# Keys and weights laid out by the host part, the order of all engines made anew, and matmuls that nothing reads ahead of the second group

## The reference, cut to what matters

```python
x = x + xattn0(ctx, layernorm(x), mask, b)     # 8 heads of 16: keys ctx[..., :128], values ctx[..., 128:]
x = x + ffn0(layernorm(x), k0, k1, k2, s0, s1, s2)          # 128 -> 512 -> 512 -> 128, weights +1/-1, relu * 2
x = x + xattn1(layernorm(x), ctx, lens, W_in, b_in, g_res, g_init)   # rmsnorm, W_in; picks a decayed patch row of ctx
x = x + ffn1(layernorm(x), W, b, Wg, bg)                    # 8 experts, the best 2 by softmax weigh in
```

## Time and profile before

| | before |
|---|---|
| time, median of 3 runs (lowest to highest) | 539.25 us (538.83 to 540.79) |
| profiled execution: its time, its span | 538.97 us, 537.2 us |
| PE, DVE, POOL, ACT busy | 497.7, 433.1, 364.5, 356.7 us |
| granted PE clock, mean | 0.982 of full speed |

### The profile page before, as it was taken

How to read it: one execution, slowest core, us unless ns; L and a number is a source line. 1 busy time by engine, 2 the same in 40 slices (tenths; PEclk the granted TensorE clock), 3 DMA queues, 4 the chain that set the end, 5 groups by cost and what they waited for, 6 DMA issues and landing times.

```text
span 537.2 us, 15110 instructions
## 1 busy us (share of the span) xinstructions
PE 497.7 (93%) x5549; PEld 324.0 (60%) x5549; DVE 433.1 (81%) x1404; ACT 356.7 (66%) x761; POOL 364.5 (68%) x633
## 2 busy tenths in 40 slices
PE   1756999999999999999999999999999999999893
PEld 1645565666656565766666566666666666655551
DVE  4735868899897979888897979799887785867897
ACT  3398698887967867677686866777566665655410
POOL 7644444588858869686868778686845857654865
PEclk9987899999999999999999999999999999999997
DMA  7402101010310101010110101000000000100010
...
DMA packets 28503, 16.98 MB, mean 32 GB/s; under 512 B 3687, under 2 KB 28429, under 8 KB 28430
## 3 DMA queue, kind: packets, MB, share of 16 engines
q1 hardware_dynamic: 26670, 15.57, 10.5%
...
## 4 chain that ended last, share of the span: by engine, by line
PE 64%; DVE 5%; issue 1%; ACT 0%; DVEq 0%
PE ps L2186 16%; PE ps L2134 16%; PE ps L2145 4%; PE ps L2079 4%; PE ps L2022 4%; PE ps L2096 4%; PE ps L2127 4%; PE ps L2164 2%; PE ps L2165 2%; PE ps L2104 2%; PE ps L2054 2%; PE ps L2177 2%; DVE weighed L1046 1%; PE ps L2083 1%; PE ps L2047 1%
## 5 line engine op out<-in xcount | busy, mean ns | idle before, releaser
L2186 PE MATMUL ps<-w_moeT,y4T 128*128 128x512 f32 x256 | 123.5, 607 | 1.2 <-DVE gd L1005 1.1
L613 POOL TENSOR_TENSOR sum<-weighed 128x512 f32<-128x512 f32 x60 | 76.1, 1269 | 71.2 <-DVE weighed L1046 71.2
L2134 PE MATMUL ps<-h,w 128*128 128x512 f16 x512 | 118.6, 379 | 0.0
L1638 ACT ACTIVATE h<-ps 128x512 f16<-128x512 f32 x128 | 74.1, 591 | 46.9 <-PE ps L2134 35.9
L1046 DVE TENSOR_TENSOR weighed<-ps,wgt 128x1024 f32<-128x1024 f32 x64 | 77.8, 1218 | 31.7 <-PE ps L2186 30.7
L969 DVE SCALAR_TENSOR_TENSOR h<-ps,h 128x512 f16<-128x512 f32 x128 | 85.6, 682 | 20.2 <-ACT h L1638 20.1
L2134 PEld LDWEIGHTS ps<-h,w 128*128 128x128 f16 x512 | 48.3, 98 | 56.2 <-issue 5.6
L1604 ACT ACTIVATE prT<-ps,maskT 77x1024 f32<-77x1024 f32 x64 | 67.3, 1101 | 14.8 <-PE ps L2083 14.5
L2186 PEld LDWEIGHTS ps<-w_moeT,y4T 128*128 128x128 f32 x256 | 45.1, 189 | 43.0 <-issue 35.0
L565 POOL TENSOR_TENSOR rs<-ve,neg_half 128x4 f32<-128x4 f32 x64 | 64.9, 1013 | 8.7
L560 POOL TENSOR_TENSOR ve<-mv,eps 128x4 f32<-128x4 f32 x64 | 14.2, 222 | 60.6 <-DVE mv L903 60.4
...
## 6 DMA issues: line engine op xcount, KB each, us to landing
...
xa<-in_x SPq DMA_DIRECT2D x16, 256.0 KB, 3.0
out_x<-xo SPq DMA_DIRECT2D x16, 256.0 KB, 2.3
...
k_u<-in_L_ffn_k ACTq DMA_DIRECT2D x1, 256.0 KB, 3.9
...
```

What stands on the lines that cost most here:

```text
L613: nc.gpsimd.tensor_tensor(sum4[:], both[:, 0:4 * D], both[:, 4 * D:8 * D], ALU.add).then_inc(c_sum4.sem, 1)
L1638: last = nc.scalar.activation(h[:, 0, (k - 1) % FC, :], src, ACT.Relu)
L2134: last = pe.matmul(pb(g, k), w2[:, i, c * 128:(c + 1) * 128], h1[:, g.p, part, i, :], start=(i == 0 and part == 0), stop=(i == FC - 1 and ...
L2186: last = pe.matmul(pm(g, j)[:, half, :], y4T[:, g.p, j * S:(j + 1) * S], w_moeT[:, half * 512:(half + 1) * 512], start=True, stop=True)
```

## The change

`kernel()` now lays out the inputs on the host: x and the output group by group, each row of a group in one piece of 2 KB; the keys of a group already turned, with zeros in the places of the other head of a pair; the values already padded, with the column of ones; the mask also turned; the expert, projection and gate weights turned and joined in one matrix, their biases in one row.

```diff
+    for h in range(H):
+        keys[:, h, :, h % HR] = grouped[..., h * HD:(h + 1) * HD].transpose(0, 3, 2, 1)
+    values[..., 0:HD] = grouped[..., D:].reshape(NG, NK, G, H, HD)
+    values[..., HD] = 1.0
+    weights = np.concatenate([w.transpose(2, 0, 1).reshape(D, -1), a["L1_xattn_W_in"].T, a["L1_ffn_Wg"].T], axis=1)
...
+            def load_keys(g):
+
+                if g.has(2):
+                    sp.wait_ge(a_less[1].sem, a_less[1].of(g, back=2))
+                sp.dma_start(kT[:, g.p], keys[g.n]).then_inc(keys_in[g.p].sem, 16)
+
+            def load_values(g):
+
+                if g.has(2):
+                    sp.wait_ge(a_pv.sem, a_pv.of(g, back=2))
+                sp.dma_start(vx[:, g.p], values[g.n]).then_inc(values_in[g.p].sem, 16)
```

```diff
+            def a_normalise(g):
+
+                dve.wait_ge(ln_a.rs.sem, ln_a.rs.of(g))
...
+                for j in range(G):
+                    last = nc.vector.tensor_scalar(xn[0][:, g.p, j * D:(j + 1) * D], xa[:, g.f, j * D:(j + 1) * D],
+                                                   mv[0][:, g.p, j, 0:1], rs[0][:, g.p, j:j + 1], ALU.subtract, ALU.mult)
+                last.then_inc(a_xn_v.sem, 1)
```

The last two groups' sums are done otherwise: DVE adds the experts of j = 1, 3 of group 14 and j = 2, 3 of group 15 one by one into the output; for j = 1 of group 15 ACT weighs, PE adds by matmuls with the identity (`e_sum`), ACT takes the result out:

```diff
+        def how(g):
+            return {NG - 2: ("gpsimd", "vector", "gpsimd", "vector"), NG - 1: ("gpsimd", "scalar", "vector", "vector")}.get(g.n, ("gpsimd",) * G)
...
+            def e_accumulate(g, j, half):
...
+                for e in range(4 * half, 4 * half + 4):
+                    so_far = xo if e else xd
+                    if e:
+                        dve.wait_ge(v_step.sem, v_steps(g, j) + e)
+                    last = nc.vector.scalar_tensor_tensor(xo[:, g.p, cols], pm(g, j)[:, e // 4, (e % 4) * D:(e % 4 + 1) * D],
+                                                          wgt[:, g.p, j, e:e + 1], so_far[:, g.p, cols], ALU.mult, ALU.add)
```

```diff
-            a_turn_keys(g[0])
+            keep_busy(12, 4)
             turn_ends()
+            keep_busy(6, 4)
             a_turn_rows(g[0])
+            keep_busy(4, 4)
             a_scores(g[0], 0)
...
-            keep_busy(4, 0)
             d_turns(g[15], (c_yT, g[15]))
-            keep_busy(4, 1)
             d_gate_scores(g[15], (c_x3, g[15]))
-            keep_busy(3, 0)
```

More of the change, by code:

```diff
@@ L60, in turned_at, with build @@
         return self.turned.of(g, self.k, back)
-def build(nc, x, ctx, mask, lens, b_attn, k0, k1, k2, s0, s1, s2, w_in, b_in, g_res, g_init, w_moe, b_moe, w_gate, b_gate, out):
-    B, S, D = x.shape
-    NK, DC = ctx.shape[1], ctx.shape[2]
+def build(nc, x, ctx, keys, values, mask, mask_turned, lens, b_attn, k0, k1, k2, s0, s1, s2, g_res, g_init, weights, biases, out):
+    B, NK = mask.shape
+    G = 4
+    NG, S, D = x.shape[0], x.shape[1], x.shape[2] // G
+    DC = ctx.shape[2] // G
     F = k0.shape[1]
     FC = F // D
-    E = w_moe.shape[0]
-    G = 4
-    NG = B // G
+    E = weights.shape[1] // D - 1
     HD = D // HEADS
@@ new lines, in count, with place, place_free @@
+        def count(kind, g, j):
+            return sum(1 for i, k in sums_of if how(i)[k] in kind and (i.n, k) <= (g.n, j))
+        def place(g, j):
+            return buffered.index((g.n, j)) % 2
+        def place_free(g, j):
+            n, k = buffered[buffered.index((g.n, j)) - 2]
+            if how(Group(n))[k] == "scalar":
+                return s_sum.sem, s_sum.of(Group(n), k + 1)
+            return c_sum4.sem, added(Group(n), k)
+        def added(g, j):
+            return count(("gpsimd",), g, j)
@@ L457, in _ @@
             plug(g[4])
[L458 to L471 removed]
+            store(g[0])
+            load_values(g[6])
+            plug(g[5])
@@ new lines, in _ @@
+            load_rows(g[8])
+            load_context(g[7])
+            store(g[1])
+            load_keys(g[7])
+            load_context(g[8])
+            plug(g[6])
+            load_values(g[7])
+            load_rows(g[9])
+            load_context(g[9])
+            plug(g[7])
+            load_keys(g[8])
+            load_context(g[10])
+            load_rows(g[10])
+            load_keys(g[9])
+            store(g[2])
+            load_values(g[8])
+            store(g[3])
+            load_values(g[9])
@@ new lines, in _ @@
+            plug(g[8])
+            load_rows(g[11])
+            load_context(g[11])
+            load_keys(g[10])
+            load_context(g[12])
+            load_values(g[10])
+            store(g[4])
+            load_rows(g[12])
+            load_keys(g[11])
+            plug(g[9])
+            load_rows(g[13])
+            plug(g[10])
+            store(g[5])
+            load_keys(g[12])
+            plug(g[11])
+            load_values(g[11])
+            store(g[6])
+            load_context(g[13])
@@ L472, in _ @@
+            load_rows(g[14])
+            load_values(g[12])
+            load_context(g[14])
+            load_keys(g[13])
+            store(g[7])
+            plug(g[12])
+            load_values(g[13])
+            load_rows(g[15])
+            load_values(g[14])
+            load_keys(g[14])
+            store(g[8])
+            load_values(g[15])
+            store(g[9])
+            load_context(g[15])
+            plug(g[13])
+            load_keys(g[15])
             store(g[10])
+            plug(g[14])
@@ new lines, in _ @@
+            e_add(g[3], 3)
+            rstd(ln_a, g[10])
+            e_out(g[3], 3)
+            e_add(g[4], 0)
+            rstd(ln_c, g[5], 1)
+            e_out(g[4], 0)
+            e_add(g[4], 1)
+            a_patch_gain(g[7])
+            rstd(ln_d, g[5])
+            e_out(g[4], 1)
+            e_add(g[4], 2)
+            rstd(ln_b, g[7])
+            e_out(g[4], 2)
+            e_add(g[4], 3)
+            a_patch_normalise(g[8])
+            e_out(g[4], 3)
+            e_add(g[5], 0)
@@ new lines, in normalise_rest @@
+            def normalise_rest(ln, g, src):
+                n, p = ln.n, g.p
+                dve.wait_ge(ln.rs.sem, ln.rs.of(g))
+                dve.wait_ge(ln.turned.sem, ln.turned_at(g, back=2))
+                for j in range(2, G):
+                    last = nc.vector.tensor_scalar(xn[n][:, p, j * D:(j + 1) * D], src[:, j * D:(j + 1) * D],
+                                                   mv[n][:, p, j, 0:1], rs[n][:, p, j:j + 1], ALU.subtract, ALU.mult)
+                last.then_inc(ln_rest[n].sem, 1)
@@ L1166, in _ @@
             b_low(g[3], 1)
+            a_picks(g[3])
+            a_split_maxima(g[5])
             b_low(g[3], 2)
@@ L1247, in _ @@
             b_low(g[6], 1)
+            a_picks(g[6])
+            a_split_maxima(g[8])
             b_low(g[6], 2)
```

1358 lines of the change are left out of this document (708 added, 650 removed).

## The result

The changed kernel takes 552.44 us (median of 4 runs, 551.53 to 552.83) against 539.27 us of the kernel before on the same chip: ratio 1.0237, 95% interval 1.0213 to 1.0261. It is slower by 2.4%. The forecast was 527.5 us, within 519 to 532.5, and 0.92 on faster.

The account below looks back on a forecast made before the run. It took latency chains through ACT at the start and DVE at the end, and PE's own work in the middle, as the bounds. Gains 3.6 + 3.3 + 4.6 = 11.5 us from 538.97 gave 527.5 us, range 519 to 532.5.

Parts of the forecast that it names:

- The failing step: At the start: counts there at 20.7, 4.6 us to write, rows 3.0 to land, so group 2 usable from 28.6 us.
- The rival on the slow side: Steady state: keys come late behind other waits in SP's list, 551.5 us at 10.5 us beyond the hidden wait; chance 0.03.
- The start: Up to `b_turns` of group 0: 46.5 to 46.9 us instead of 50.08, a gain of 3.6 us, bounds 0 and 7.5.
- The wait for group 2's rows: At the start: late rows of group 2 hold back all of PE's list for about 5 us.
- The 37 matmuls: At the start: matmuls that nothing reads, 14 us at most, placed where PE had nothing, so costing nothing.
- The 2.6 us for the early matmuls at full clock: At the start: PE at full instead of half clock for two halves of scores and one of weights, 2.6 us less.
- the rival on POOL and DVE: At the start: POOL and DVE get in each other's way, 5 us on the path, 532.5 us in all; chance 0.04.
- The middle: PE-bound stretch: groups 4 to 15 no longer turn keys, 0.27 us each, 3.3 us less; new order counted as 0.
- the experts moved behind `b_last`: PE's experts (13, 2) moved behind `b_last` of group 15: 1.8 us earlier, 0.8 given back, 1.0 gained.
- The end: From `b_last` of group 15 to the end: 5.3 us of savings taken as 3.6; with the moved experts, 4.6.
- The forecast's case: Whole kernel: the main prediction, a time of 523 to 530.5 us; chance 0.61.
- only the turns count: Whole kernel: late rows and keys and serial 0.5 us steps cancel the start's and end's gains, 533.5 us; chance 0.15.

Follow-up runs that it names:

- e4: The changed kernel with the load of w_T's 127 rows issued as two loads, 112 and 15 rows: 534.55 us, ratio 0.9922.
- e7: The changed kernel with w_T's 127 rows loaded as 126 rows and 1 row: 533.05 us, ratio 0.9874.
- e8: The kernel before the change with its load of the experts' weights, 128 rows, issued as 127 rows and 1 row: 550.60 us, ratio 1.0205.
- e13: The changed kernel with w_T's 127 rows still in one load, but issued by ACT instead of SP: 552.31 us, ratio 1.0242.
- e9: e5 with two expert weighings moved ahead of picks and maxima splits in DVE's list: 532.52 us, ratio 0.9869.
- e11: e5 with the sum of experts (15, 2) at the end moved from DVE to ACT and PE: 532.79 us, ratio 0.9883.
- e12: e5 with PE's experts (13, 2) put back ahead of b_last of group 15: 533.44 us, ratio 0.9882.
- e10: e5 with the end's 17 matmuls that nothing reads put back where the kernel before had them: 532.84 us, ratio 0.9870.
- e14: e5 with the edits of e10 and e11 together: 533.14 us, ratio 0.9891.
- e6: e4 without the 37 matmuls of the start that nothing reads: 535.35 us, ratio 0.9928.
- e5: e4 with the rows of groups 2 and 3 moved ahead of the weights' loads and counts in SP's list: 534.38 us, ratio 0.9908.

## Why the prediction was wrong, point by point

- **The failing step** is the sentence "with two issues, group 2 can be looked at from 28.6". It counted what stands in SP's list by the length of an issue. `load_weights` stands ahead of `order_counts` and was given no price at all: seven loads, of which the first, by its 127 rows, keeps one DMA engine at work until 41 us (6.3% of 16 engines' time, one piece each 0.18 us). The rows were there at 46.3, 17.7 us late; with the split of e4 they are issued at 25.75 and DVE starts on them at 29.76. Shown by e4 and e7 (cured by the split), e8 (the fault put into the kernel before) and e13 (the same fault by another queue). Size: `b_turns` 15.3 us later than before instead of 3.6 earlier. That is 18.9 of the 25.2 us by which the profiled execution missed the forecast; the stretch from `b_turns` to `xc` has 2.8 of the rest (1.5 less than before, where 4.3 were forecast) and the end 3.3 (0.3 less, where 3.6 were forecast).
- **The rival on the slow side** had the right kind of cause, a load late in SP's list, at the wrong place. "Nothing in the list stands behind a wait of that length that I can find" was true of semaphores and not of the queue; in the steady state no key was late. That its 551.5 us lies near the 552.4 measured is chance.
- **The start without the fault**: counted from the first scores, 1.8 to 2.9 us are gained (e4 to e7, e9, e11, e12) and nothing in e10 and e14, where the steps gave 3.6. The wait for group 2's rows was forecast as some 5 us and is 3.2. From the first scores to the values 3.6 to 4.6 us are gained in six of these (3.0 in e6, 1.3 to 1.5 in e10 and e14), not 6.4. "The 37 matmuls lie in time in which PE had nothing" is wrong: five of them hold back the turned maxima, 0.7 us in e5, 1.7 in the changed kernel, 2.1 in e10. The 2.6 us for the early matmuls at full clock were counted without that, and no run shows them; the runs show 7.8 us instead of 10.1 from the turned maxima to the values (e5, e6) and first mask rows of 0.32 us instead of 0.45, and in the time of e6 what is left of this is not told from zero. DVE's normalise of group 2 was priced at 0.8 us and takes 2.10 (1.11 for group 3 in e4), while POOL works beside it: this is in small what the rival on POOL and DVE feared, though no run shows that POOL is the cause. The sign weights were priced at 3.5 us and take 2.2.
- **The middle** was forecast at 3.3 less, and 1.0 for the experts moved behind `b_last`. From `b_turns` of group 0 to `xc` of group 15 stood 452.1 us; e4, e6 and e9, without a dip there, take 449.0 to 449.7: 2.4 to 3.1 less. Of these 1.7 belong to the moved experts (e12), 0.4 of which come back behind `xc`. The steady period gives 0.22 to 0.23 a group, near the forecast's 0.27, some 2.7 in all; two waits for DVE, 3.7 us where the kernel before had 1.1, take back 2.6 of it. These terms give 1.8, and the rest of the 2.4 to 3.1 is open. I had taken 0 for the order, bounds -3 and +4.
- **The end** was forecast at 3.6 less behind `b_last`; without a dip it is 1.5 (33.5 us in e4, 35.0 before). `xc` to `xd` 0.4 longer and not 0.7 shorter, as DVE's half of the normalise stands behind a weighing, and `xd` waits 0.58 for POOL; `xd` to `wgt` 0.5 longer and not 1.5 shorter, as half of `e_accumulate(14, 3)` stands ahead of `d_top`; behind `wgt` 2.4 less and not 3.1. A step of `e_accumulate` takes 0.40 from start to start (541.99 to 545.22 for eight), not 0.33.
- **The sum** with the fault cured: e4 to e7 take 533.1 to 535.4 us. The forecast's case was 523 to 530.5; even then "only the turns count" (533.5; its own sum gives 533.7) would have been the nearest, though its reason, late keys and steps of 0.5 us, did not come.
